# The output products of an FFN split into three fp32r terms, with streamed weight parts and low parts made by GpSimd

## The reference

```python
q, k, v = heads(x, Wq, bq), heads(x, Wk, bk), heads(x, Wv, bv)        # 16 heads of 16
qp = relu(einsum('bhsd,hdf->bhsf', q, rw)) + EPS                       # 64 features
kp = relu(einsum('bhsd,hdf->bhsf', k, rw)) + EPS
kv = einsum('bhsf,bhsd->bhfd', kp, v)                                  # sums over a whole sequence
out = einsum('bhsf,bhfd->bhsd', qp, kv) / (einsum('bhsf,bhf->bhs', qp, kp.sum(axis=2)) + EPS)
```

```python
w = einsum('btd,bthkd->bthk', h, down_embed[idx])
w = silu(w) * softmax(scores)                          # 4 heads x 8 chosen experts
experts = einsum('bthk,bthkd->btd', w, up_embed[idx])
mlp = silu(h @ Wg + bg) * (h @ Wu + bu) @ Wd + bd      # 1024 hidden columns
out = layernorm(h + mlp + experts)
```

## Time and profile before

| | |
|---|---|
| median of 3 runs | 3519.4 us (3515.91 to 3520.86) |
| the profiled execution's own time | 3515.04 us |
| its span | 3513.3 us, so 1.7 us lie around it |
| busy: PE, DVE, ACT, POOL | 97%, 81%, 57%, 33% |
| mean granted TensorE clock | 0.991 |

### The profile page before, as it was taken

How to read it: one execution, slowest core, us unless ns; L and a number is a source line. 1 busy time by engine, 2 the same in 40 slices (tenths; PEclk the granted TensorE clock), 3 DMA queues, 4 the chain that set the end, 5 groups by cost and what they waited for, 6 DMA issues and landing times.

```text
span 3513.3 us, 49408 instructions
## 1 busy us (share of the span) xinstructions
PE 3414.6 (97%) x18400; PEld 2693.9 (77%) x18400; DVE 2830.2 (81%) x5316; ACT 1990.0 (57%) x2886; POOL 1163.0 (33%) x724
## 2 busy tenths in 40 slices
PE   8779999999999999999999999999999999999988
PEld 6457877777877777877777877777777778777777
DVE  4688888888888888888888887888878888888873
ACT  4456556555566555556555655555655564555551
POOL 0233333333333333333333333333333333343330
PEclk9899999999999999999999999999999999999999
DMA  4000000000000000000000000000000000000000
GB/s 121 18 13 19 7 13 19 19 19 19 7 13 19 19 19 14 12 13 19 19 19 9 17 13 19 19 19 7 19 13 19 19 13 7 13 13 7 12 7 12
DMA packets 23452, 60.84 MB, mean 17 GB/s; under 512 B 5808, under 2 KB 10160, under 8 KB 23216
## 3 DMA queue, kind: packets, MB, share of 16 engines
q1 hardware_dynamic: 23216, 57.69, 5.0%
HBM read 40.91 MB, written 16.78 MB: 16 GB/s over the span
## 4 chain that ended last, share of the span: by engine, by line
PE 81%; DVE 8%; ACT 6%; issue 3%; POOL 2%; DMA 0%; SPq 0%; POOLq 0%; DVEq 0%; ACTq 0%
PE ring L651 25%; PE y_bank L744 11%; PE y_bank L746 10%; PE step_bank L553 6%; PE step_bank L545 5%; PE step_bank L651 4%; PE step_bank L589 3%; PE step_bank L581 3%; PE step_bank L680 3%; DVE prob L1144 3%; PE step_bank L670 3%; PE step_bank L724 3%; PE step_bank L539 2%; POOL grid L464 2%; PE y_bank L740 1%
## 5 line engine op out<-in xcount | busy, mean ns | idle before, releaser
L464 POOL TENSOR_TENSOR grid<-ex 128x1024 f32<-128x1024 f32 x512 | 997.6, 1956 | 1507.5 <-ACT ex L877 730.6
L744 PE MATMUL y_bank<-wd_sb,gate 128*128 128x256 f32 x2048 | 622.3, 386 | 1.7 <-DVE wexp L1166 1.7
L746 PE MATMUL y_bank<-up_sb,wexp 128*128 128x256 f32 x2048 | 609.1, 379 | 0.0
L1144 DVE SCALAR_TENSOR_TENSOR prob<-grid,narrow,prob 128x1024 f32<-128x1024 f32 x256 | 552.2, 2157 | 9.0
L651 PE MATMUL ring<-x1T_hl,downT_hl 128*128 128x512 f32 x1536 | 420.8, 409 | 16.8 <-ACT gate L901 16.7
L651 PE MATMUL ring<-x1T_hl,wg_hl 128*128 128x512 f32 x1536 | 431.2, 416 | 3.8 <-DVE gate L1160 3.8
L1131 DVE SCALAR_TENSOR_TENSOR grid<-grid,best 128x1024 f32<-128x1024 f32 x256 | 327.2, 1278 | 131.8 <-POOL grid L464 128.8
L746 PEld LDWEIGHTS y_bank<-up_sb,wexp 128*128 128x128 f32 x2048 | 389.2, 190 | 53.0
L651 PE MATMUL ring<-x1T_hl,wu_hl 128*128 128x512 f32 x1536 | 421.4, 409 | 0.0
L744 PEld LDWEIGHTS y_bank<-wd_sb,gate 128*128 128x128 f32 x2048 | 354.0, 190 | 53.3 <-issue 25.2
L651 PEld LDWEIGHTS ring<-x1T_hl,wu_hl 128*128 128x128 f32 x1536 | 282.0, 188 | 119.8 <-issue 42.9
(11 more groups left out here) (169 smaller groups left out, 5578.7 us busy)
## 6 DMA issues: line engine op xcount, KB each, us to landing
xb<-in_L_attn_x SPq DMA_DIRECT2D x34, 512.0 KB, 3.5
out_y<-x SPq DMA_DIRECT2D x32, 512.0 KB, 2.9
xa<-in_L_attn_x SPq DMA_DIRECT2D x30, 512.0 KB, 4.2
prob<-in_L_ffn_down_embed SPq DMA_DIRECT2D x1, 1024.0 KB, 6.0
prob<-in_L_ffn_Wg SPq DMA_DIRECT2D x1, 1024.0 KB, 8.8
prob<-in_L_ffn_Wu SPq DMA_DIRECT2D x1, 1024.0 KB, 10.9
wd_sb<-in_L_ffn_Wd SPq DMA_DIRECT2D x1, 1024.0 KB, 11.3
up_sb<-in_L_ffn_up_embed SPq DMA_DIRECT2D x1, 1024.0 KB, 11.8
```

Of the source, the lines that this page charges most:

```text
L464: pool.tensor_tensor(grid[:, h % 2], bcast(ex[:, h, 0:NX].unsqueeze(2), [P, NX, NK]), bcast(ex[:, RH + h, 0:NK].unsqueeze(1), [P, NX, NK]) ...
L744: pe.matmul(rows, gate[:, c % 2, t * P:(t + 1) * P], wd_sb[:, c, :], start=(c == 0 and t % 2 == 0), stop=False, skip_group_check=True)
L746: mm = pe.matmul(rows, wexp[:, c % 2, t * P:(t + 1) * P], up_sb[:, c, :], start=False, stop=(c == C - 1), skip_group_check=True)
L1144: ins = dve.scalar_tensor_tensor(out=row, in0=g, scalar=rz[:, h:h + 1], in1=row, op0=ALU.mult, op1=ALU.add, accum_out=mass[:, 0:1] if h == ...
```

## The change

Both output products are taken in three terms of fp32r operands, high x high, high x low and low x high, six matmuls of 128 x 256 for each tile and chunk in place of two fp32 ones.

- Weights: at the start, ACT and DVE split `Wd` and `up_embed` into high and low parts (in steps that run beside the fill of the pipeline), SP stores them to device memory (`wdup_kept`). In the loop, GpSimd issues for every chunk a load of 128 x 4 x 256 values (512 KB) into one of two buffers `wdup`. `wd_sb` and `up_sb` are gone.
- The moving side of the chain: ACT makes the high part of `gate` (`gate_top`) behind its Silu of the dots and of `wexp` (`wexp_top`) behind its Silu of the next gate. For chunks 0 to 6 GpSimd makes the low parts (`ff_low`, 128 x 512 each): that of `gate` at the end of its step, that of `wexp` in the next step ahead of the spreads. Chunk 7's two are made by DVE, with `ff_wexp(7)` moved ahead of `keep(3, 2)`.
- The unsplit `gate` and `wexp` now lie in parts of `prob` that are free at the time; new waits (`wexp_split`, `last_split`) keep the masks of ACT from writing there too early.

```diff
+        wdup = sb("wdup", P, 2, 4, D, dt=F32R)
+        wdup_kept = nc.dram_tensor("wdup_kept", [C, P, 4, D], F32).ap()
...
@@ SP, at the start @@
+            for w, i in [(0, 0), (0, 1), (0, 2), (0, 3), (1, 0), (1, 1), (1, 2), (1, 3)]:
+                sp.wait_ge((wd_low, up_low)[w], i + 1)
+                sp.dma_start(wdup_kept[2 * i:2 * i + 2, :, 2 * w:2 * w + 2, :].rearrange("c p w d -> p c w d"),
+                             wdup[:, :, 2 * w:2 * w + 2, :].bitcast(F32)).then_inc((wd_kept, up_kept)[w], 16)
@@ GpSimd @@
+                def ff_low(whole, high, low, s_high, s_split, c):
+                    pool.wait_ge(s_high, n * C + c + 1)
+                    pool.tensor_tensor(low[:, c % 2], whole(par, c), high[:, c % 2].bitcast(F32),
+                                       ALU.subtract).then_inc(s_split, 1)
+
+                def ff_stream(c):
+
+                    g = n * C + c
+                    if g == 0:
+                        pool.wait_ge(wd_kept, 16 * (C // 2))
+                        pool.wait_ge(up_kept, 16 * (C // 2))
+                    wait(pool, y_full, g - 1)
+                    pool.dma_start(wdup[:, c % 2], wdup_kept[c]).then_inc(wdup_loaded[c % 2], 16)
+
                 for c in range(C):
                     t, odd = divmod(c, 2)
                     kv_adds(KV_FIRST[c])
+                    if ff:
+                        ff_stream(c)
+                    if ff and c:
+                        ff_low(wexp, wexp_hi, wexp_lo, wexp_high, wexp_split, c - 1)
                     if rt and odd:
                         spread(t, 2)
...
                     if rt and not odd:
                         spread(t, 1)
+                    if ff and c < C - 1:
+                        ff_low(gate, gate_hi, gate_lo, gate_high, gate_split, c)
@@ TensorE @@
-                        pe.wait_ge(h_ready, n * C + c + 1)
-                        pe.wait_ge(*drained("pt", n, c))
+                        pe.wait_ge(wdup_loaded[c % 2], 16 * ((n * C + c) // 2 + 1))
+                        if c == C - 1:
+                            pe.wait_ge(last_split, 2 * (n + 1))
+                        else:
+                            pe.wait_ge(gate_split, n * (C - 1) + c + 1)
+                            pe.wait_ge(wexp_split, n * (C - 1) + c + 1)
...
-                        pe.matmul(rows, gate[:, c % 2, t * P:(t + 1) * P], wd_sb[:, c, :],
-                                  start=(c == 0 and t % 2 == 0), stop=False, skip_group_check=True)
-                        mm = pe.matmul(rows, wexp[:, c % 2, t * P:(t + 1) * P], up_sb[:, c, :],
-                                       start=False, stop=(c == C - 1), skip_group_check=True)
+                        terms = [(gate_hi, 0), (gate_hi, 1), (gate_lo, 0), (wexp_hi, 2), (wexp_hi, 3), (wexp_lo, 2)]
+                        for i, (src, w) in enumerate(terms):
+                            mm = pe.matmul(rows, src[:, c % 2, t * P:(t + 1) * P], wdup[:, c % 2, w, :],
+                                           start=(c == 0 and t % 2 == 0 and i == 0), stop=(c == C - 1 and i == 5),
+                                           skip_group_check=True)
@@ ScalarE @@
+                def gate_top(c):
+                    act.wait_ge(h_ready, n * C + c + 1)
+                    act.copy(gate_hi[:, c % 2], gate(par, c)).then_inc(gate_high, 1)
+
+                def wexp_top(c):
+                    act.wait_ge(*drained("pt", n, c))
+                    act.copy(wexp_hi[:, c % 2], wexp(par, c)).then_inc(wexp_high, 1)
...
                     if ff:
                         ff_gate(c)
+                        if c:
+                            wexp_top(c - 1)
...
                     if ff:
                         ff_dots(c)
+                        gate_top(c)
...
+                    if ff and c == C - 1:
+                        wexp_top(c)
@@ VectorE @@
+                def ff_low(whole, high_part, low_part, s_high, c):
+                    dve.wait_ge(s_high, n * C + c + 1)
+                    low(low_part[:, c % 2], whole(par, c), high_part[:, c % 2], last_split)
...
+                    if ff and c == C - 1:
+                        ff_wexp(c)
+                        ff_low(gate, gate_hi, gate_lo, gate_high, c)
                     if rt and odd:
                         keep(t, 2)
...
-                    if ff:
+                    if ff and c == C - 1:
+                        ff_low(wexp, wexp_hi, wexp_lo, wexp_high, c)
+                    if ff and c < C - 1:
                         ff_wexp(c)
```

More of the change, by code:

```diff
@@ L801, in prep @@
                 bank = banks[k % 2]
+                for i in PREP_WD.get(k, ()):
+                    act.wait_ge(wd_staged, 16)
+                    wait(act, wd_kept, 16 * i)
+                    act.copy(wdup[:, :, 0, :], wd_rows[:, 2 * i:2 * i + 2, :]).then_inc(wd_high, 1)
+                for i in PREP_UP.get(k, ()):
+                    act.wait_ge(up_staged, 16)
+                    wait(act, up_kept, 16 * i)
+                    act.copy(wdup[:, :, 2, :], up_rows[:, 2 * i:2 * i + 2, :]).then_inc(up_high, 1)
+                if k > PREP_WU:
+                    return
                 if k < PREP_WG:
@@ L893, in mask @@
                         act.wait_ge(*full("pt", s - 2, C - 1))
+                        act.wait_ge(wexp_split, (s - 1) * (C - 1))
+                        act.wait_ge(last_split, 2 * (s - 1))
+                    if t == 2 and h == 0 and ff:
+                        act.wait_ge(wexp_split, n * (C - 1) + C // 2)
                     act.wait_ge(bent, s * (ACT_HEADS * T) + t * ACT_HEADS + h + 1)
@@ L900, in ff_gate @@
                     wait(act, y_full, n * C + c - 1)
-                    act.activation(gate[:, c % 2], ring[c % 2][:], ACT.Silu,
+                    if c == 0:
+                        wait(act, last_split, 2 * n)
+                    act.activation(gate(par, c), ring[c % 2][:], ACT.Silu,
                                    bias=bg_sb[:, c:c + 1]).then_inc(ring_act, 1)
@@ L905, in ff_dots @@
                     act.wait_ge(ring_full, n * (3 * C) + 3 * c + 3)
-                    act.activation(wexp[:, c % 2], ring[c % 2][:], ACT.Silu).then_inc(ring_act, 1)
+                    act.activation(wexp(par, c), ring[c % 2][:], ACT.Silu).then_inc(ring_act, 1)
+                def gate_top(c):
[4 more added lines that the diff above has]
+                    act.copy(wexp_hi[:, c % 2], wexp(par, c)).then_inc(wexp_high, 1)
                 for c in range(C):
@@ L973, in prep @@
                     low(wu_hl[:, 1], wu_rows, wu_hl[:, 0], low_ready)
+                for i in PREP_WD.get(k, ()):
+                    dve.wait_ge(wd_high, i + 1)
+                    low(wdup[:, :, 1, :], wd_rows[:, 2 * i:2 * i + 2, :], wdup[:, :, 0, :], wd_low)
+                for i in PREP_UP.get(k, ()):
+                    dve.wait_ge(up_high, i + 1)
+                    low(wdup[:, :, 3, :], up_rows[:, 2 * i:2 * i + 2, :], wdup[:, :, 2, :], up_low)
             def lows(blocks, half, bank, bias, high, group):
@@ L1159, in ff_h @@
                     dve.wait_ge(ring_act, n * (2 * C) + 2 * c + 1)
-                    dve.scalar_tensor_tensor(out=gate[:, c % 2], in0=ring[1 - c % 2][:], scalar=bu_sb[:, c:c + 1],
-                                             in1=gate[:, c % 2], op0=ALU.add, op1=ALU.mult).then_inc(h_ready, 1)
+                    dve.scalar_tensor_tensor(out=gate(par, c), in0=ring[1 - c % 2][:], scalar=bu_sb[:, c:c + 1],
+                                             in1=gate(par, c), op0=ALU.add, op1=ALU.mult).then_inc(h_ready, 1)
                 def ff_wexp(c):
```

37 lines of the change are left out of this document (28 added, 9 removed).

## The result

The changed kernel takes 3803.93 us (median of 4 runs, 3798.17 to 3805.83) against 3518.17 us (median of 4): a ratio of 1.0809, 95% interval 1.079 to 1.0828. It is 8.1% slower, outside the range, and no rival reached it. The profiled execution has a span of 3803.4 us.

A forecast was written before the change was run, and what follows sets the result against it. PE was taken as the bound, DVE next. Cheaper matmuls save 160 us, leaving PE at 3355; DVE's work, stops and kept waits make 3438, giving back 83. Forecast 3440 us, range 3345 to 3565.

The forecast's parts named there:

- The matmuls: Output matmuls on PE: six fp32r take 0.705 us per tile and chunk against 0.86, saving 160 us.
- Starting work: Splitting and storing the weights at the start, beside the pipeline's filling: costs nothing; without that cover about 10 us.
- The high parts on ACT: 512 copies on ACT, 301 us, bring it to 68% and are hidden as load; POOL's third spread comes 0.6 us later.
- The weight loads: 256 loads of 512 KB issued by POOL a step ahead: hidden, with issuing near 0.33 us each.
- The low parts on POOL: 448 low parts at 1.15 us each; POOL's load of 1763 us is hidden, its place in the chain not.
- The stops of DVE: POOL's low parts stop DVE in 5.6 of 14 cases per group: 206 us, bounds nothing and 533.
- The sum: DVE's 3079 us busy, 321 of waiting and 38 of short waits give 3438, against 3355 for PE.
- The last sentence of the prediction: If PE and DVE, tied by two banks, didn't smooth each other's stops, both are paid and the change is slower.
- Rival 2: POOL's chain, with low parts and load ahead of even chunks' outputs, stops PE: 3520 to 3630 us, likely 3560, chance 0.26.

The follow-up runs named there:

- e5: e2 with DVE writing its two products rounded to fp32r directly, so ACT makes no high parts: 3440.13 us, ratio 0.9789.
- e6: e5 with weight parts loaded only for chunks 0 and 1, which serve all chunks: 3442.94 us, ratio 0.9792.
- e8: e6 plus 14 unneeded 128 x 512 subtractions for each group on GpSimd, at the low parts' places, nobody waiting: 3600.76 us, ratio 1.024.
- e2: The changed kernel with no low parts of gate or wexp made; PE takes high parts instead, still six matmuls: 3624.22 us, ratio 1.0301.
- e1: The changed kernel with all low parts still made, but PE waits only for high parts and uses those instead: 3835.92 us, ratio 1.0905.

## Why the prediction was wrong

- **The matmuls** (160 us): right. 0.685 us for a tile and chunk against 0.705 forecast. In e5 PE's busy time in the 24 passes falls by 4.6 us each, against 5 forecast. The span of e5 is 76 us shorter: 94 in those passes and 11 behind them, and the head takes 28 back. That e5 takes 3440 us, the number forecast for the whole change, is chance: it has neither high parts on ACT nor low parts.
- **Starting work** ("cost nothing; without that cover about 10 us"): wrong. 28.7 us, and 38 until the fourth group. I counted the splits' durations, not that each waits for a store to land, nor SP's queue behind them. The queue of the engine that issues belongs into the account of a start, and I had left SP's out.
- **The high parts on ACT** ("as a load they are hidden"; behind `gate_top` stand "the middle uses of the attention stage and the exponentials, of which the latter wait for DVE anyway"): this is the step that failed most plainly. I named the middle uses and gave them no price; they are what frees PE's banks. Measured: 184 us without low parts, 95 of it by place, and by the estimate above about 72 by ACT's time as such.
- **The weight loads**: right, hidden, as far as e6 shows it. The issue costs POOL 0.6 us, not 0.33, and this is hidden too.
- **The low parts on POOL** (1.15 us, at most 1.19): too low, 1.28 and 1.32 in the median. The 1.32 that the prediction worked out beside it was the better value. The bound was half of a longer addition that writes fp32, while this one writes fp32r; which of the two makes the difference no run tells.
- **The stops of DVE** (206 us): the size is right in e8 (206) and too small for the changed kernel, where DVE's busy time rises by 288, of which 46 are its own two low parts for each group and 242 the rest. The 206 is met partly by luck. I had 5 of 5.6 hits at the experts' selection, some 184 us, where e8 has 123 and the changed kernel 131, and 0.6 of a hit at the norm's writes, some 22 us, where they have 64 and 132.
- **The sum**: wrong in its form. I made one engine's account, DVE's work and waits against PE's, and took the larger. The last sentence of the prediction named this danger and gave it no chance of its own. DVE kept its idle time (685 us), PE's grew from 10 to 212 in the 24 passes, and both were paid. So the low parts cost 180 us (e2 to the changed kernel) where the sum has 83 for them (3438 - 3355), and the high parts 184 where it has nothing. Rival 2 gave up to 3630 for the chain through POOL and was wrong in its mechanism: its waits were there, 7.2 us for a group, and taking them away (e1) brought nothing.
- **What no term held**: the granted clock. The same 20448 matmuls are 3396.6 us of PE's busy time here and 3282.2 in e5. The mean clock is 0.958 against 0.983. An estimate from these, (1 - 0.958) x 3803 - (1 - 0.983) x 3437, gives 101 us if PE was busy throughout the slow stretches, so matmuls at the lower level, such as those at 1966.33, make most of the 114; the rest isn't taken apart. In the rows shown the lower level stands behind a stop of PE, so I take it for a thing that makes stops dearer and not for a cause of its own; no run holds the clock fixed.

The parts, each measured against its neighbour: e5 to e2, +184 for the high parts; e2 to the changed kernel, +180 for the low parts, where POOL's instructions alone make 158 in another surrounding. With e5's 78 below the kernel before, that is the 286. Of the 83 us behind the 24 passes I haven't taken apart what belongs to which; a window of the same stretch is 22 us above the kernel before in e2 and 55 in e8, so GpSimd's instructions have the larger part.

## What to carry to other kernels

When several engines work in a fixed order and are tied by a few banks, don't compare loads: for each instruction added to an engine, write down what stands behind it there and who waits for that, and give it a price even where its own engine is at 60%. A wait shown in the profile isn't a cost until a run without it is faster: here taking away 231 us of TensorE's waits alone brought nothing, and 72 us came from copies for which nobody waited. The splits went here through engines on the chain, and that cost more than the cheaper matmuls brought. The product that makes the value rounded it for nothing (0.751 and 0.684 us in the median in e5, as before), but that gives the high part alone.

## What the runs showed of the hardware

- GpSimd and VectorE hold each other up for whole instructions: VectorE's write of 128 x 256 from SBUF to SBUF with two scalars takes 0.40 us alone, 1.88 in the median here, 3.84 at most; a GpSimd subtraction of 1.26 us at least takes up to 2.28.
- GpSimd's subtraction of 128 x 512 fp32 into fp32r takes 1.28 or 1.32 us in the median; its issue of a 512 KB load 0.60 us in the median, with 3.6 us to landing.
- An fp32r matmul of 128 x 256 with its own weights starts every 0.114 us (1.37 / 12), an fp32 one every 0.43.
- The granted clock was 0.50 behind a stop of PE of 2.59 us in the changed kernel and behind one of 2.37 in e2: 2.90 us for twelve matmuls at 1966.33, 1.41 at 1972.65. The Trainium skill (TensorE: Matmul & The Clock Gate, What's actually happening) has the two levels, 1.2 and 2.4 GHz; the rows agree, with a ratio of 2.90 / 1.41 = 2.06.
